# Routed blocks of an expert layer worked in groups of three, and down weights laid over 96 partitions

## The chip, the cores and the metric

The kernel runs on one core of a Trainium2 chip, as one program. Its engines are PE (TensorE: matmuls, with their weight loads shown as PEld), DVE (VectorE), ACT (ScalarE), POOL (GpSimd) and SP (SyncE, which here only issues transfers). The metric is the device time of one execution in microseconds (us). The kernel before took 770.0 us, the median of three runs (769.4 to 772.3).

## The reference, cut to what matters

The program is two transformer layers on x of 4 x 256 tokens of width 256; each layer is a cross-attention and a feed-forward with experts. The change touches only the last part, the experts of the second layer:

```python
# 1024 tokens, H = 256, E = 60 experts, I = 176, TOP_K = 4, all float32
probs = softmax(x @ gate_w.T);  weights, sel = top_k(probs, 4)
cw = zeros((M, E)).at[arange(M)[:, None], sel].add(weights)
def step(acc, ews):                        # scanned over the 60 experts
    w13_e, w2_e, cw_e = ews                # w13: 352 x 256, w2: 256 x 176
    gu_e = x @ w13_e.T
    h = silu(gu_e[:, :I]) * gu_e[:, I:]
    return acc + cw_e[:, None] * (h @ w2_e.T), None
return shared + sparse                     # shared: a dense expert of width 704
```

The kernel does not multiply every token with every expert. It gives each expert slots of token rows, gathers the rows, works them, and scatters the results back.

## The kernel before, in words

The rows sent to the 60 experts are laid out in 53 blocks of 128 rows. Blocks 0 to 44 come in threes for four experts: two blocks with two experts of 64 rows each, then one block with the 32 further rows of all four (`tenants`, line 1697). Blocks 45 to 52 (one round of 8) hold what is over, two units of 64 rows each with an expert known only at run time. Further rounds stand behind a branch at the end and are skipped here.

What one block b goes through in `routed_l1`:

- POOL gathers its 128 rows of 1 KB from `x_rows` into `xg` by an indirect transfer (`fetch_rows`, L1761). There are `XBUF` = 11 such buffers, and fetches run `FETCH` = 8 blocks ahead: POOL's order is fetch(8), send(0), fetch(9), send(1), and so on, so that fetch(b + 8) stands behind send(b - 1) on POOL (L2118 to L2121).
- PE turns the rows (`turn_x`, two transposes, L2138); ACT copies them to SBUF (L2203).
- PE multiplies by the gate and up weights (`gate_up`, L2152). Each expert takes its own columns of the array, 64 or 32 of them, and the products of a block's experts run side by side. ACT applies silu (L2209), and DVE multiplies the halves (L2234).
- PE turns the result in two pieces of 88 columns (`turn_hid`, L2161); ACT copies (L2215).
- PE multiplies by the down weights (`outputs`, L2174), again in column tiles. DVE weights the rows into one of `YBUF` = 4 buffers `yb` (L2245), and POOL scatters them to `y_rows` (L2115).

On PE the blocks are interleaved: step b issues turn_x(b + 3), gate_up(b + 2), turn_hid(b + 1) and outputs(b). So full transposes and column-tiled products alternate, four changes to a block. ACT and DVE follow the same order.

The weights of two experts (a pair) come by two transfers from SP (`load_weights`, L1731): gate and up on 128 partitions, down on 88 partitions (`HC`). A ring holds 12 pairs. Pairs 0 to 11 are loaded before the stage begins; pair q goes out when the last block of pair q - 12 has been multiplied (L2099), two pairs at the end of every three blocks. Pairs 30 to 37, for the last 8 blocks, are loaded expert by expert from a run-time index (`load_further`, L1742).

Behind the last block, POOL waits until all scatters have landed; then the rows of a token are read back, added and stored (`combine_and_store`).

Of the kernel before, what the change touches and what calls it, by code (L numbers as in the profile page):

```python
# [18 lines left out]
P = 128  # L19
D = 256  # L20
# [1638 lines left out]
HC = I1 // 2  # L1659

# [18 lines left out]
XBUF, YBUF, FETCH = 11, 4, 8  # L1679
# [33 lines left out]
def pair_last(q):  # L1713

    return 3 * (q // 2) + 2 if 2 * q < E1 else BASE + q - E1 // 2

# [48 lines left out]
def route_shared_l1(nc, m, io, block, ctx):  # L1765
# [37 lines left out]
    sw13, sw2 = sb("sw13", [KD, 2 * I1S]), sb("sw2", [CH, D])  # L1803
    m.over_ready, m.shared_read, m.y_copied, m.added = sem("over_ready"), silu_done, y_copied, added
# [247 lines left out]
def routed_l1(nc, m, io, block, ctx, out):  # L2052
# [18 lines left out]
    def all_rounds(eng, ahead, step):  # L2071

        for b in range(FIRST - ahead):
            step(b, FIRST)
        eng.wait_ge(m.over_ready, 1)
        units = eng.value_load(m.over[0:1, 0:1], min_val=0, max_val=OVER)

        def further(r):
            end = FIRST + r * ROUND
            if r == FURTHER:  # L2080
                for b in range(end - ahead, end):
                    step(b, end)
                return
            with eng.If(units > 2 * (r + 1) * ROUND):
                for b in range(end - ahead, end + ROUND - ahead):
                    step(b, end + ROUND)
                further(r + 1)
            with eng.Else():
                for b in range(end - ahead, end):
                    step(b, end)  # L2090

        further(0)

    @block.sync
    def _(sp):
# [8 lines left out]
        all_rounds(sp, ROUND, load)  # L2104

    @block.gpsimd
    def _(pool):
# [19 lines left out]
        all_rounds(pool, FETCH, step)  # L2127
# [3 lines left out]
    def _(pe):  # L2131

        def turn_x(b):
            pe.wait_ge(x_loaded[b % XBUF], 16 * (b // XBUF + 1))
            if b >= 2:
                pe.wait_ge(xt_done, b - 1)
            for c in range(KD):
                ins = nc.tensor.transpose(ps[:, 6 + b % 2, c * P:(c + 1) * P], xg[:, b % XBUF, c * P:(c + 1) * P],  # L2138
                                          m.ident[:])
            ins.then_inc(xt_ps, 1)  # L2140

        def gate_up(b):
# [49 lines left out]
        gate_up(0)  # L2192
        gate_up(1)
        turn_hid(0)
        all_rounds(pe, 3, step)

    @block.scalar
    def _(act):
        def copy_x(b):
            act.wait_ge(xt_ps, b + 1)  # L2200
            if b >= 4:
                act.wait_ge(gu_ps, b - 3)
            nc.scalar.copy(xgT[:, b % 4, :], ps[:, 6 + b % 2, 0:D]).then_inc(xt_done, 1)  # L2203

        def silu(b):
            act.wait_ge(gu_ps, b + 1)
            if b >= 2:
                act.wait_ge(hid_done, b - 1)
            nc.scalar.activation(act_g[:, b % 2, :], ps[:, b % 2, 0:I1], ACT.Silu).then_inc(silu_done, 1)  # L2209

        def step(b, end):
            act.wait_ge(ht_ps, b + 1)
            if b >= 2:
                act.wait_ge(y_ps, b - 1)
            nc.scalar.copy(hidT[:, b % 2, :], ps[0:HC, 2 + b % 2, 0:2 * P]).then_inc(ht_done, 1)  # L2215
            if b + 3 < end:
                copy_x(b + 3)
            if b + 2 < end:
                silu(b + 2)

        for b in range(3):
            copy_x(b)
        m.last_copies()
        silu(0)
        silu(1)
        all_rounds(act, 3, step)

    @block.vector
    def _(dve):
        def multiply(b):  # L2230
            dve.wait_ge(silu_done, b + 1)
            if b >= 2:
                dve.wait_ge(ht_ps, b - 1)
# [188 lines left out]
```

## Time and profile before

| | us |
|---|---|
| median of 3 runs (lowest, highest) | 770.0 (769.4, 772.3) |
| the profiled execution, device time | 778.58 |
| span of its trace | 776.8 |
| first product of the routed stage (L2152) | at 584.11 |
| first weight load that waits for the ring | at 596.62 |
| last down product of the stage (L2174) ends | at 751.17 |
| last scatter issued, all landed | at 754.82, 757.31 |

The profiled execution is 8.6 us longer than the median. The trace gives each instruction's start and length on its engine, in microseconds from the start of the span, with its line in the kernel and the tiles it writes and reads. A window row adds up the busy time of each engine in a stretch, with the clock that PE was granted, the mean busy share of the 16 DMA engines and the bytes moved. Idle time is put down to what ended it; "issue" means that the engine waited for nothing that the profile shows.

### The profile page before, as it was taken

Reading aid. Unit: us, or ns where it says so; the run is one execution under the profiler, and the core shown is the slowest. Engines: PE = TensorE matmul, PEld = TensorE weight load, DVE = VectorE, ACT = ScalarE, POOL = GpSimd, SP = SyncE. Lnnn points to the kernel's source line nnn. Section 1 sums busy time; section 2 is a strip of 40 time slices with the busy share of each in tenths; the row PEclk is TensorE's granted clock in tenths of the full one; section 3 lists DMA queues with packets and bytes.
Section 4 is the critical chain, followed back from the end, with each engine's and each line's share of the span. In section 5 each row is a group of like instructions: output and inputs, shape, how many; then the busy total and the mean of one; then the engine's idle time right before and its main releaser. Section 6 shows DMA issues by size and latency. Waiting matters only on the chain. (4 is left out here: it accounts for less than half of the span.)

```text
span 776.8 us, 12603 instructions
## 1 busy us (share of the span) xinstructions
PE 658.9 (85%) x4224; PEld 377.0 (49%) x4224; DVE 427.4 (55%) x1148; ACT 304.9 (39%) x606; POOL 253.7 (33%) x403
## 2 busy tenths in 40 slices
PE   1757888886899999998569999599999999999960
PEld 1543444443676766765335555455664444443430
DVE  4658888863412668868586654469952222222226
ACT  1333778874232223422147676331224332322210
POOL 5350111111144323222102333022365565656530
PEclk9785999998599999999669999689999999999995
DMA  3086211100600556553803310493013999999817
GB/s 114 3 279 187 61 55 57 44 3 1 172 0 14 148 156 183 167 185 108 187 18 109 84 44 1 98 297 126 0 45 103 296 275 280 276 262 292 281 69 270
DMA packets 81807, 103.86 MB, mean 134 GB/s; under 512 B 10093, under 2 KB 56514, under 8 KB 81738
## 3 DMA queue, kind: packets, MB, share of 16 engines
q1 hardware_dynamic: 73930, 85.31, 37.8%
q0 software_dynamic: 5600, 14.02, 6.1%
q10 hardware_dynamic: 2208, 3.67, 1.3%
q8 instruction: 36, 0.59, 0.3%
q14 instruction: 33, 0.27, 0.1%
HBM read 81.17 MB, written 21.65 MB: 132 GB/s over the span
## 5 line engine op out<-in xcount | busy, mean ns | idle before, releaser
L769 DVE TENSOR_REDUCE l_mx<-ps 128x2 f32<-128x512 f32 (+2 forms) x256 | 125.7, 550 | 45.6 <-PE ps L629 45.3
L857 ACT ACTIVATE l_prob<-ps 128x1024 f32<-128x1024 f32 x96 | 98.5, 1027 | 25.8 <-PE ps L659 25.6
L629 PE MATMUL ps<-l_ks,l_qs 48*128 48x256 bf16 (+1 forms) x384 | 71.1, 298 | 28.4 <-DMA l_qs<-l_q_stacks 14.2
L1392 DVE SCALAR_TENSOR_TENSOR xs<-ps,comb,xs 128x256 f32<-128x256 f32 x128 | 55.8, 481 | 59.3 <-PE ps L1052 59.2
L2115 POOL DMA_INDIRECT y_rows<-r_at_blk,row x53 | 52.3, 987 | 59.4 <-DVE r_at_blk L2245 51.9
L674 PE MATMUL ps<-l_prob,v 128*9 128x256 f32 (+1 forms) x768 | 70.3, 389 | 1.1 <-ACT l_prob L857 1.1
L2234 DVE TENSOR_TENSOR r_hot<-r_hot,ps 128x176 f32<-128x176 f32 x53 | 17.9, 338 | 82.5 <-ACT r_hot L2209 43.9
L1141 POOL TENSOR_TENSOR r_ehid<-r_erelu 128x512 f32<-128x512 f32 x32 | 35.5, 1109 | 83.6 <-ACT r_erelu L1245 83.6
L1052 PE MATMUL ps<-f_w,r_ehid 128*128 128x256 f32 x256 | 60.8, 380 | 0.2
L1041 PE MATMUL ps<-xT,f_w 128*128 128x512 f32 x128 | 60.0, 592 | 0.0
L1761 POOL DMA_INDIRECT xg<-x_rows,r_empty x53 | 53.1, 1002 | 18.8 <-issue 14.5
L1052 PEld LDWEIGHTS ps<-f_w,r_ehid 128*128 128x128 f32 x256 | 48.4, 190 | 21.1 <-issue 13.9
L629 PEld LDWEIGHTS ps<-l_ks,l_qs 48*128 48x128 bf16 (+1 forms) x384 | 29.4, 102 | 59.4 <-issue 21.9
L659 PE MATMUL ps<-l_qs,l_ks 50*128 50x256 bf16 (+1 forms) x384 | 56.3, 280 | 0.0
L2245 DVE TENSOR_SCALAR r_at_blk<-ps,row_w 128x256 f32<-128x256 f32 x53 | 25.6, 483 | 51.5 <-remote 24.8
L597 POOL TENSOR_TENSOR attn<-rest,l_rec 128x32 f32<-128x32 f32 x64 | 14.4, 246 | 114.1 <-DVE l_rec L788 114.1
L597 POOL TENSOR_TENSOR l_ctxv<-rest,l_rec 128x64 f32<-128x64 f32 x64 | 17.7, 297 | 85.2 <-DVE l_rec L788 85.2
L2203 ACT COPY r_at_low<-ps 128x256 f32<-128x256 f32 x53 | 19.7, 373 | 59.4 <-PE ps L2138 33.9
L2152 PE MATMUL ps<-ew,r_at_low 128*64 128x352 f32 (+1 forms) x304 | 40.9, 468 | 2.3 <-issue 2.3
L1847 PE MATMUL ps<-xT,r_sw 128*128 128x512 f32 x88 | 41.7, 614 | 0.0
L674 PEld LDWEIGHTS ps<-l_prob,v 128*9 128x9 f32 (+1 forms) x768 | 26.8, 98 | 23.0 <-issue 10.2
L2209 ACT ACTIVATE r_hot<-ps 128x176 f32<-128x176 f32 x53 | 16.9, 320 | 51.9 <-PE ps L2152 25.5
(278 smaller groups left out, 1132.3 us busy)
## 6 DMA issues: line engine op xcount, KB each, us to landing
ew<-in_L_w SPq DMA_DIRECT2D x18, 704.0 KB
ew13b<-in_L_w SPq DMA_DIRECT2D x12, 704.0 KB
f_w<-in_L_w SPq DMA_DIRECT2D x32, 256.0 KB, 2.9
ew<-in_L_w SPq DMA_DIRECT2D x22, 352.0 KB
ew2b<-in_L_w SPq DMA_DIRECT2D x12, 352.0 KB
ew13b<-in_L_w SPq DMA_DIRECT2D x12, 352.0 KB
l_k_stacks<-part SPq DMA_DIRECT2D x8, 384.0 KB, 3.4
l_ks<-l_k_stacks SPq DMA_DIRECT2D x32, 96.0 KB, 2.3
```

The costliest lines, as they stand in the source:

```text
L629: ins = nc.tensor.matmul(ps[:, score_bank(n) + k, qt * S:(qt + 1) * S], qs[row:row + R, u % NBUF, col, qt * P:(qt + 1) * P], ks[row:row + ...
L659: ins = nc.tensor.matmul(ps[:, 2 + 2 * (n % 2) + k, kt * S:(kt + 1) * S], ks[row:row + lay.krows, b, col, kt * P:(kt + 1) * P], qs[row:row ...
L674: ins = nc.tensor.matmul(ps[row:row + W, 6, (c % 2) * S:(c % 2 + 1) * S], v[:, n // UP // GR * QT + kt, head, :], prob[:, n % PROBS, k, kt ...
L769: ins = nc.vector.reduce_max(mx[:, u % 2, :, s, head], one[:, :, lo:hi], AX_X)
L857: nc.scalar.activation(prob[:, n % PROBS, :, :, :].rearrange("p h k q -> p (h k q)"), ps[:, 2 + 2 * (n % 2):4 + 2 * (n % 2), :].rearrange( ...
L1041: ins = nc.tensor.matmul(m.ps[:, n % 2, :], m.f0_up[:, n % WSLOTS, c, :], m.xT[:, c, half * HT:(half + 1) * HT], start=(c == 0), stop=(c = ...
L1052: nc.tensor.matmul(m.ps[:, 2 + t, 0:D], ehid[:, n % 2, t * P:(t + 1) * P], m.f0_down[:, n % WSLOTS, :], start=True, stop=True).then_inc(e_ ...
L1392: v.scalar_tensor_tensor(m.xs[:, i, :], m.ps[:, 2 + t, 0:D], m.comb[:, i, e:e + 1], m.xs[:, i, :], ALU.mult, ALU.add).then_inc(e_added, 1)
L1761: nc.gpsimd.indirect_dma_start(m.xg[:, b % XBUF, :], None, m.x_rows, bass.IndirectOffsetOnAxis(m.token[:, b:b + 1], 0)).then_inc(m.x_loade ...
L1847: ins = nc.tensor.matmul(ps[:, 2 * (q % 2) + a, :], sw13[:, k, own], m.xT[:, k, h * TILES * P:(h + 1) * TILES * P], start=(k == 0), stop=( ...
L2115: nc.gpsimd.indirect_dma_start(m.y_rows, bass.IndirectOffsetOnAxis(m.row[:, b:b + 1], 0), yb[:, b % YBUF, :], None).then_inc(y_sent[b % YB ...
L2152: ins = nc.tensor.matmul(ps[row:row + n, b % 2, 0:2 * I1], xgT[:, b % 4, c * P + row:c * P + row + n], w13[:, s, c, :], start=(c == 0), st ...
```

## The change

Blocks are worked in groups of three (`group_blocks`: 15 groups of three, then 3, 3 and 2 for the round of 8). In step g, PE issues turn_x for the three blocks of group g + 1, turn_hid for the three of group g, then the products that have two experts per block (gate_up of group g + 1, outputs of group g), then those with four experts per block, in the same way. ACT copies and applies silu over two blocks at once and then over the third (`parted`); DVE multiplies likewise, while it weights block by block. PSUM is laid out anew for three blocks at a time: rows turned for a third block share their place with a third block's output, so turn_x of it waits for `y_done` of the group before. `yb` moves to the buffer of the shared expert's weights and has 6 places for 4. Down weights are padded in DRAM and SBUF from 88 to 96 partitions; the products read 88. `FETCH`, `XBUF`, POOL's order and the ring of weights stay.

```diff
 HC = I1 // 2
+HCP = 96
...
-XBUF, YBUF, FETCH = 11, 4, 8
+XBUF, YBUF, FETCH = 11, 6, 8
+GROUPS_ROUND = -(-ROUND // 3)
+FIRST_GROUPS = BASE // 3 + GROUPS_ROUND
...
+def group_blocks(g):
+    if g < BASE // 3:
+        return range(3 * g, 3 * g + 3)
+    r, k = divmod(g - BASE // 3, GROUPS_ROUND)
+    first = BASE + r * ROUND
+    return range(first + 3 * k, min(first + 3 * k + 3, first + ROUND))
+
+
+def spot(b):
+
+    k = b if b < BASE else (b - BASE) % ROUND
+    return k % 3
+
+
+def parted(blocks):
+
+    return [p for p in (blocks[0:2], blocks[2:3]) if len(p)]
+
+
+def halves(b):
+
+    whole, k = (0, b) if b < BASE else divmod(b - BASE, ROUND)
+    done = 2 * (b // 3) if b < BASE else 2 * (BASE // 3) + whole * (2 * (ROUND // 3) + (ROUND % 3 > 0)) + 2 * (k // 3)
+    return done + (1 if spot(b) < 2 else 2)
...
-    xgT = at_low.rearrange("p (j d) -> p j d", j=4)
-    act_g, hid = (hot[:, a * 2 * I1:(a + 1) * 2 * I1].rearrange("p (j n) -> p j n", j=2) for a in range(2))
-    hidT = hot[0:HC, 4 * I1:4 * I1 + 4 * P].rearrange("p (j n) -> p j n", j=2)
-    yb = at_blk[:, 0:YBUF * D].rearrange("p (j d) -> p j d", j=YBUF)
+    xgT = at_low[:, 0:3 * D].rearrange("p (j d) -> p j d", j=3)
+    act_g, hid = (hot[:, a * 3 * I1:(a + 1) * 3 * I1].rearrange("p (j n) -> p j n", j=3) for a in range(2))
+    hidT = hot[0:HC, 6 * I1:6 * I1 + 6 * P].rearrange("p (j n) -> p j n", j=3)
+    yb = m.sw2
...
+    x_ps = (ps[:, 6, 0:D], ps[:, 6, D:2 * D], ps[:, 7, 0:D])
+    hid_ps = (ps[0:HC, 3, 0:D], ps[0:HC, 3, D:2 * D], ps[0:HC, 5, 0:D])
+    out_ps = (ps[:, 4, 0:D], ps[:, 4, D:2 * D], ps[:, 7, 0:D])
...
-        def turn_x(b):
+        def turn_x(b, sent):
             pe.wait_ge(x_loaded[b % XBUF], 16 * (b // XBUF + 1))
-            if b >= 2:
-                pe.wait_ge(xt_done, b - 1)
+            if spot(b) == 2 and sent:
+                pe.wait_ge(y_done, sent)
             for c in range(KD):
-                ins = nc.tensor.transpose(ps[:, 6 + b % 2, c * P:(c + 1) * P], xg[:, b % XBUF, c * P:(c + 1) * P],
+                ins = nc.tensor.transpose(x_ps[spot(b)][:, c * P:(c + 1) * P], xg[:, b % XBUF, c * P:(c + 1) * P],
                                           m.ident[:])
             ins.then_inc(xt_ps, 1)
 
@@ -2143,111 +2178,131 @@
             q = pair_first(b)
             if q is not None:
                 pe.wait_ge(m.ew_loaded[q % (RING // 2)], ring_loads(q))
-            pe.wait_ge(xt_done, b + 1)
-            if b >= 2:
-                pe.wait_ge(hid_done, b - 1)
+            pe.wait_ge(xt_done, halves(b))
             for c in range(KD):
                 for row, n, w in tenants(b):
                     w13, _, s = ring_slot(m, w)
-                    ins = nc.tensor.matmul(ps[row:row + n, b % 2, 0:2 * I1], xgT[:, b % 4, c * P + row:c * P + row + n],
+                    ins = nc.tensor.matmul(ps[row:row + n, spot(b), 0:2 * I1],
+                                           xgT[:, spot(b), c * P + row:c * P + row + n],
                                            w13[:, s, c, :], start=(c == 0), stop=(c == KD - 1))
             ins.then_inc(gu_ps, 1)
 
         def turn_hid(b):
-            pe.wait_ge(hid_done, b + 1)
-            if b >= 2:
-                pe.wait_ge(ht_done, b - 1)
+            pe.wait_ge(hid_done, halves(b))
+            if b == 2:
+                pe.wait_ge(m.y_copied, NT)
             for c in range(2):
-                ins = nc.tensor.transpose(ps[0:HC, 2 + b % 2, c * P:(c + 1) * P],
-                                          hid[:, b % 2, c * HC:(c + 1) * HC], m.ident[:])
+                ins = nc.tensor.transpose(hid_ps[spot(b)][:, c * P:(c + 1) * P],
+                                          hid[:, spot(b), c * HC:(c + 1) * HC], m.ident[:])
             ins.then_inc(ht_ps, 1)
 
         def outputs(b):
-            pe.wait_ge(ht_done, b + 1)
-            if b == 0:
-                pe.wait_ge(m.y_copied, NT)
-            if b >= 2:
-                pe.wait_ge(y_done, b - 1)
+            pe.wait_ge(ht_done, halves(b))
+            if b >= 3:
+                pe.wait_ge(y_done, b - spot(b))
             for c in range(2):
                 for row, n, w in tenants(b):
                     _, w2, s = ring_slot(m, w)
-                    ins = nc.tensor.matmul(ps[row:row + n, 4 + b % 2, 0:D], hidT[:, b % 2, c * P + row:c * P + row + n],
-                                           w2[:, s, c, :], start=(c == 0), stop=(c == 1))
+                    ins = nc.tensor.matmul(out_ps[spot(b)][row:row + n, :], hidT[:, spot(b), c * P + row:c * P + row + n],
+                                           w2[0:HC, s, c, :], start=(c == 0), stop=(c == 1))
             ins.then_inc(y_ps, 1)
 
-        def step(b, end):
-            if b + 3 < end:
-                turn_x(b + 3)
-            if b + 2 < end:
-                gate_up(b + 2)
-            if b + 1 < end:
-                turn_hid(b + 1)
-            outputs(b)
+        def step(g, end):
+            ahead = group_blocks(g + 1) if g + 1 < end else ()
+            for b in ahead:
+                turn_x(b, group_blocks(g)[0])
+            for b in group_blocks(g):
+                turn_hid(b)
+            for many in (2, 4):
+                for b in ahead:
+                    if len(tenants(b)) == many:
+                        gate_up(b)
+                for b in group_blocks(g):
+                    if len(tenants(b)) == many:
+                        outputs(b)
 
         pe.wait_ge(m.table_read, 1)
-        for b in range(3):
-            turn_x(b)
+        for b in group_blocks(0):
+            turn_x(b, 0)
         m.last_outputs()
         pe.wait_ge(m.shared_read, UNITS)
-        gate_up(0)
-        gate_up(1)
-        turn_hid(0)
-        all_rounds(pe, 3, step)
+        for b in group_blocks(0):
+            gate_up(b)
+        all_rounds(pe, FIRST_GROUPS, GROUPS_ROUND, 1, step)
 
...
     @block.scalar
     def _(act):
...
+        def copy_x(bs):
+            p, n = spot(bs[0]), len(bs)
+            act.wait_ge(xt_ps, bs[-1] + 1)
+            if bs[0] >= 3:
+                act.wait_ge(gu_ps, bs[0] - p)
+            nc.scalar.copy(xgT[:, p:p + n, :].rearrange("p j d -> p (j d)"), ps[:, 6 + p // 2, 0:n * D]
+                           ).then_inc(xt_done, 1)
+
...
+        def step(g, end):
+            ahead = group_blocks(g + 1) if g + 1 < end else ()
+            for bs in parted(ahead):
+                copy_x(bs)
+            for bs in parted(group_blocks(g)):
+                copy_hid(bs)
+            for bs in parted(ahead):
+                silu(bs)
+
...
     @block.vector
     def _(dve):
...
+        def weighted(b, last):
+            dve.wait_ge(y_ps, last + 1)
             if b >= YBUF:
                 dve.wait_ge(y_sent[b % YBUF], 16 * (b // YBUF))
+            nc.vector.tensor_scalar(yb[:, b % YBUF, :], out_ps[spot(b)], m.row_w[:, b:b + 1], None,
                                     ALU.mult).then_inc(y_done, 1)
 
-        multiply(0)
-        multiply(1)
-        all_rounds(dve, 2, step)
...
+        def step(g, end):
+            ahead = parted(group_blocks(g + 1) if g + 1 < end else ())
+            for k, bs in enumerate(parted(group_blocks(g))):
+                if k < len(ahead):
+                    multiply(ahead[k])
+                for b in bs:
+                    weighted(b, bs[-1])
+            for bs in ahead[len(parted(group_blocks(g))):]:
+                multiply(bs)
+
...
-        m.ew2 = m.sb("ew2", [HC, EARLY, 2, D])
+        m.ew2 = m.sb("ew2", [HCP, EARLY, 2, D])
...
-            m.ew2b = m.sb("ew2b", [HC, RING - EARLY, 2, D], ctx=scope)
+            m.ew2b = m.sb("ew2b", [HCP, RING - EARLY, 2, D], ctx=scope)
...
-    io["L1_w2"] = rows_together(io.pop("L1_ffn_w2").transpose(0, 2, 1), HC)
+    io["L1_w2"] = np.pad(rows_together(io.pop("L1_ffn_w2").transpose(0, 2, 1), HC), ((0, 0), (0, HCP - HC), (0, 0)))
```

PE in the middle of the stage, before: xg holds gathered rows, r1_hot the silu and its product, r1_at_low the turned rows, ew13 and ew2 the weights; a row's last field is the shape of one matmul.

```order
L2138 MATMUL ps<-ident,xg 128x128 x2
L2152 MATMUL ps<-ew13,r1_at_low 64x352 x4
L2161 MATMUL ps<-ident,r1_hot 88x128 x2
L2174 MATMUL ps<-ew2,r1_hot 32x256 x8
L2138 MATMUL ps<-ident,xg 128x128 x2
L2152 MATMUL ps<-ew13,r1_at_low 32x352 x8
L2161 MATMUL ps<-ident,r1_hot 88x128 x2
L2174 MATMUL ps<-ew2,r1_hot 64x256 x4
```

The same place after, one whole step:

```order
L2173 MATMUL ps<-ident,xg 128x128 x6
L2195 MATMUL ps<-ident,r1_hot 88x128 x6
L2185 MATMUL ps<-ew13,r1_at_low 64x352 x8
L2206 MATMUL ps<-ew2,r1_hot 64x256 x8
L2185 MATMUL ps<-ew13,r1_at_low 32x352 x8
L2206 MATMUL ps<-ew2,r1_hot 32x256 x8
```

Two blocks before had eight stretches of four kinds; three blocks after have six stretches, and all turns of rows stand at the head of the step.

PE at the end of the stage, before:

```order
L2138 MATMUL ps<-ident,xg 128x128 x2
L2152 MATMUL ps<-ew13,r1_at_low 64x352 x4
L2161 MATMUL ps<-ident,r1_hot 88x128 x2
L2174 MATMUL ps<-ew2b,r1_hot 64x256 x4
L2152 MATMUL ps<-ew13,r1_at_low 64x352 x4
L2161 MATMUL ps<-ident,r1_hot 88x128 x2
L2174 MATMUL ps<-ew2b,r1_hot 64x256 x4
L2161 MATMUL ps<-ident,r1_hot 88x128 x2
L2174 MATMUL ps<-ew2,r1_hot 64x256 x8
```

The same place after:

```order
L2173 MATMUL ps<-ident,xg 128x128 x4
L2195 MATMUL ps<-ident,r1_hot 88x128 x6
L2185 MATMUL ps<-ew13,r1_at_low 64x352 x8
L2206 MATMUL ps<-ew2b,r1_hot 64x256 x12
L2195 MATMUL ps<-ident,r1_hot 88x128 x4
L2206 MATMUL ps<-ew2,r1_hot 64x256 x8
```

The gate and up products of the last two blocks now stand ahead of the outputs of the three blocks before them.

## Rows read from the trace of the kernel before

**Rows 1.** Windows of core 0: window, length, busy (x count) per engine, clock, DMA share, GB/s
```profile
512.00:524.00 12.00, 12.00 (x45) 5.63 (x44) 9.69 (x35) 4.42 (x7) 3.94 (x3) 0.99 1.05 263
527.00:533.00 6.00, 6.00 (x19) 3.42 (x18) 5.72 (x10) 1.07 (x2) 1.78 (x1) 1.00 0.72 240
600.00:735.00 135.00, 131.32 (x1062) 55.03 (x1058) 33.15 (x82) 39.72 (x124) 81.31 (x83) 1.00 0.97 282
```

**Rows 2.** Waits from 590 to 762 us: engine line waited for, us, times, longest
```profile
PEld ps L2138 <- issue: 19.3, 49, 0.4
...
PE ps L2152 <- issue: 2.7, 4, 2.0
```

**Rows 3.** Timeline, 655 to 675 us, one block on PE: start, us, engine, instruction
```profile
656.57 0.44 PE L2138 MATMUL ps<-ident,xg 128*128 128x128 f32 x2
...
656.94 1.41 PE L2152 MATMUL ps<-ew,r_at_low 128*64 128x352 f32 x8
...
658.27 0.42 PE L2161 MATMUL ps<-ident,r_hot 128*88 128x128 f32 x2
...
658.62 1.08 PE L2174 MATMUL ps<-ew,r_hot 88*64 88x256 f32 x8
...
659.64 0.44 PE L2138 MATMUL ps<-ident,xg 128*128 128x128 f32 x2
659.75 0.48 DVE L2245 TENSOR_SCALAR r_at_blk<-ps,row_w 128x256 f32<-128x256 f32 x1 [0.68 <-PE ps L2174]
```

**Rows 4.** Timeline, 655 to 675 us, from a weighted block to POOL's transfers
```profile
655.41 0.48 DVE L2245 TENSOR_SCALAR r_at_blk<-ps,row_w 128x256 f32<-128x256 f32 x1 [2.45 <-remote]
...
656.18 0.99 POOL L2115 DMA_INDIRECT y_rows<-r_at_blk,row  x1 [1.63 <-DVE r_at_blk L2245]
...
657.47 0.97 POOL L1761 DMA_INDIRECT xg<-x_rows,r_empty  x1 [0.30 <-issue]
...
658.74 0.99 POOL L2115 DMA_INDIRECT y_rows<-r_at_blk,row  x1 [0.30 <-issue]
```

**Rows 5.** Timeline, 572 to 612 us, the first blocks on PE
```profile
580.92 0.60 PE L2138 MATMUL ps<-ident,xg 128*128 128x128 f32 x4
...
584.11 2.59 PE L2152 MATMUL ps<-ew,r_at_low 128*64 128x352 f32 x16
...
586.63 0.42 PE L2161 MATMUL ps<-ident,r_hot 128*88 128x128 f32 x2
```

**Rows 6.** DMA issues from 500 to 536 us: KB each, median us to landing
```profile
ew13b<-in_L_w SPq DMA_DIRECT2D x6, 704.0 KB
ew2b<-in_L_w SPq DMA_DIRECT2D x6, 352.0 KB
...
r_sw<-in_L_shared_w SPq DMA_DIRECT2D x3, 256.0 KB, 7.2
r_sw<-in_L_shared_w SPq DMA_DIRECT2D x1, 128.0 KB, 6.5
```

**Rows 7.** Line 1761, the row fetches: ns min/median/max, first and last start
```profile
L1761 POOL DMA_INDIRECT xg<-x_rows,r_empty x53: 952/970/1873, 566.6 to 731.7; - x53
```

**Rows 8.** Timeline of the sync engine: its weight loads
```profile
596.62 21.65 SPq L1731 DMA_DIRECT2D ew<-in_L_w  x12
...
719.18 10.27 SPq L1742 DMA_DIRECT2D ew<-in_L_w  x8
```

**Rows 9.** Chain of waits at the stage's end: start, us, what
```profile
743.28 0.37 PE ps L2138 x2
...
746.35 2.02 issue
...
750.13 1.04 PE ps L2174 x8
...
754.82 2.49 DMA y_rows<-r_at_blk,row
```

More of the change, by code:

```diff
@@ L1803, in route_shared_l1 @@
     sw13, sw2 = sb("sw13", [KD, 2 * I1S]), sb("sw2", [CH, D])
+    m.sw2 = sw2
     m.over_ready, m.shared_read, m.y_copied, m.added = sem("over_ready"), silu_done, y_copied, added
@@ L2069, in routed_l1, with all_rounds @@
     ps = m.ps
-    def all_rounds(eng, ahead, step):
-        for b in range(FIRST - ahead):
-            step(b, FIRST)
+    x_ps = (ps[:, 6, 0:D], ps[:, 6, D:2 * D], ps[:, 7, 0:D])
+    hid_ps = (ps[0:HC, 3, 0:D], ps[0:HC, 3, D:2 * D], ps[0:HC, 5, 0:D])
+    out_ps = (ps[:, 4, 0:D], ps[:, 4, D:2 * D], ps[:, 7, 0:D])
+    def all_rounds(eng, first, size, ahead, step):
+        for n in range(first - ahead):
+            step(n, first)
         eng.wait_ge(m.over_ready, 1)
@@ L2078, in further @@
         def further(r):
-            end = FIRST + r * ROUND
+            end = first + r * size
             if r == FURTHER:
-                for b in range(end - ahead, end):
-                    step(b, end)
+                for n in range(end - ahead, end):
+                    step(n, end)
                 return
             with eng.If(units > 2 * (r + 1) * ROUND):
-                for b in range(end - ahead, end + ROUND - ahead):
-                    step(b, end + ROUND)
+                for n in range(end - ahead, end + size - ahead):
+                    step(n, end + size)
                 further(r + 1)
             with eng.Else():
-                for b in range(end - ahead, end):
-                    step(b, end)
+                for n in range(end - ahead, end):
+                    step(n, end)
         further(0)
@@ L2103, in load @@
                     load_further(sp, m, io, 2 * q)
-        all_rounds(sp, ROUND, load)
+        all_rounds(sp, FIRST, ROUND, ROUND, load)
     @block.gpsimd
@@ L2126, in _ @@
         pool.wait_ge(m.added, NT)
-        all_rounds(pool, FETCH, step)
+        all_rounds(pool, FIRST, ROUND, FETCH, step)
         nc.gpsimd.memset(settled_mark, 0.0).then_inc(y_settled, 1)
@@ L2205, in silu @@
[L2205 to L2219, printed above, removed]
@@ L2221, in _, with copy_hid @@
-        for b in range(3):
-            copy_x(b)
+        def copy_x(bs):
[5 more added lines that the diff above has]
+                           ).then_inc(xt_done, 1)
+        def copy_hid(bs):
+            p, n = spot(bs[0]), len(bs)
+            act.wait_ge(ht_ps, bs[-1] + 1)
+            if bs[0] >= 3:
+                act.wait_ge(y_ps, bs[0] - p)
+            src = ps[0:HC, 3, 0:2 * D] if p == 0 else hid_ps[p]
+            nc.scalar.copy(hidT[:, p:p + n, :].rearrange("p j d -> p (j d)"), src).then_inc(ht_done, 1)
@@ new lines, in silu @@
+        def silu(bs):
+            p, n = spot(bs[0]), len(bs)
+            act.wait_ge(gu_ps, bs[-1] + 1)
+            if bs[0] >= 3:
+                act.wait_ge(hid_done, halves(bs[0] - p - 1))
+            nc.scalar.activation(act_g[:, p:p + n, :], ps[:, p:p + n, 0:I1], ACT.Silu).then_inc(silu_done, 1)
+        def step(g, end):
[6 more added lines that the diff above has]
+                silu(bs)
@@ L2223, in _ @@
+        for bs in parted(group_blocks(0)):
+            copy_x(bs)
         m.last_copies()
-        silu(0)
-        silu(1)
-        all_rounds(act, 3, step)
+        for bs in parted(group_blocks(0)):
+            silu(bs)
+        all_rounds(act, FIRST_GROUPS, GROUPS_ROUND, 1, step)
     @block.vector
     def _(dve):
[L2230 to L2233, printed above, removed]
-            nc.vector.tensor_tensor(hid[:, b % 2, :], act_g[:, b % 2, :], ps[:, b % 2, I1:2 * I1], ALU.mult
-                                    ).then_inc(hid_done, 1)
@@ L2237, in _, with multiply @@
-        m.clear_sems(dve)
-        def step(b, end):
-            if b + 2 < end:
-                multiply(b + 2)
-            dve.wait_ge(y_ps, b + 1)
+        def multiply(bs):
+            p, n = spot(bs[0]), len(bs)
+            dve.wait_ge(silu_done, halves(bs[0]))
+            if bs[0] >= 3:
+                dve.wait_ge(ht_ps, bs[0] - p)
+            nc.vector.tensor_tensor(hid[:, p:p + n, :], act_g[:, p:p + n, :], ps[:, p:p + n, I1:2 * I1], ALU.mult
+                                    ).then_inc(hid_done, 1)
@@ new lines, in step @@
+        def step(g, end):
[7 more added lines that the diff above has]
+                multiply(bs)
+        for bs in parted(group_blocks(0)):
+            multiply(bs)
+        all_rounds(dve, FIRST_GROUPS, GROUPS_ROUND, 1, step)
```

7 lines of the change are left out of this document (1 added, 6 removed).

## The prediction

> **What bounds the kernel now.** The change touches only the stretch from the first routed product at 584.11 us [rows 5] to the last scatter [rows 9], so I read that alone. First the windows, for who is busy: from 600 to 735 us PE works 131.3 of 135 us at full clock, and the 16 DMA engines are busy 0.97 of the time at 282 GB/s, while DVE, ACT and POOL have room [rows 1]. Two things are close to full at once. Then the waits, for which of the two ends last: the row turns never stood over 0.4 us, the products waited 2.7 us in all, and neither waited for a DMA [rows 2]. So PE sets the pace, and the weights come in time. Then the timeline, for what PE spends on a block: from one row turn to the next 3.06 us, made of 0.37 (turn of the rows), 1.33 (gate and up), 0.35 (turn of the hidden) and 1.01 (down) [rows 3]. Three blocks cost 9.19.
>
> The stage runs from 584.11 to 751.17 [rows 5, 9]. Its pieces are 2.52 for the first two gate-up products, 0.35, fifty blocks with all four parts (153.0), and 2.69 + 1.36 + 1.01 for the last blocks without turns: 160.9. With the stand of 2.0 us at the branch [rows 9] that is 162.9; the other 4.2 us are scattered stalls.
>
> **The change, part by part.** *Trains on PE.* Four row turns in a train took 0.60 [rows 5], 0.15 each, where a pair alone takes 0.37, so a change of kind costs 0.07 there. Six of them: 0.97. Six hidden turns at the same pace: 0.90. Two gate-up products in a train took 2.52 (584.11 to 586.63, rows 5) for 2 x 1.33, so the change into products costs about 0.15. I take it once for each train and let the down products follow without it, at 1.01 - 0.15 = 0.86. A step of three blocks is then 0.97 + 0.90 + 2.52 + 1.72 + 1.33 + 0.86 = 8.30 instead of 9.19. The bounds are 9.19, if every change still costs, and 7.9, if none does. Were PE still the bound, 17 steps would save 15 us.
>
> *What is late next: the gathered rows.* FETCH stays 8 while the rows are turned earlier, all at the head of a step. The last block turned in step g is 3g + 5; its fetch stands on POOL behind the send of block 3g - 4, the last of group g - 2. Counted from the start of step g - 2: the two-expert outputs end at 0.97 + 0.90 + 2.52 + 1.72 = 6.11; DVE starts 0.12 later (a product from 658.62 that takes 1.01, DVE at 659.75, rows 3); POOL's send follows 0.77 after DVE's start, and each POOL transfer is 1.28 behind the last [rows 4]. Send, fetch, send, fetch, send, fetch: the third fetch goes out at 7.00 + 5 x 1.28 = 13.4. It must have landed when step g has turned two blocks, at two steps plus 0.67. So two steps are 12.7 plus the landing time, and a step is 6.37 plus half of it.
>
> The trace does not show that landing time. From below it is 2.5, what the last scatter, also 128 KB, took with nothing else moving [rows 9]. From above it is 11.6: the last fetch went out at 731.7 and its rows were turned at 743.28 without a wait [rows 7, 9]. Nearest are loads of 128 and 256 KB while DMA was full, 6.5 and 7.2 [rows 6]. I take 7.0, since DMA is full here too, with both kinds of queue. A step is then 9.87, longer than the 9.19 of today; the two are equal at 5.6 us. PE waits 1.57 in each step, with the hidden turns and all the products queued behind the row turn, and with them ACT, DVE and the next sends.
>
> *Weights.* A pair is 704 + 352 KB [rows 6] and becomes 704 + 384. The loads that wait for the ring begin at 596.62 [rows 8], 26 pairs, after the third block as now. They are 26 x 1.114 = 29.0 MB, and about 90 row transfers of 128 KB add 11.8: 40.8 MB, at 282 GB/s 145 us, to 741. With the steps below, the last pairs are wanted from 743 on, so they are just covered. If the cover goes, the outputs of three blocks stand behind the wait, which they did not before.
>
> When 88-partition loads drain alone, the mean share is 0.72, which is 11.5 of 16 engines, at 240 GB/s; with all at work it was 263 [rows 1]. The spread over 96 may thus be worth up to a tenth of the rate; in the stage the share is already 0.97, so I count nothing, and the bounds on the end of the loads are 730 and 752 (at 305, which is 282 x 1.05 / 0.97, and at 263 GB/s).
>
> The Trainium skill (DMA: Bandwidth & Descriptors, section "Why a DMA increments its semaphore by 16 and not by 1") says that a load is split over the largest number up to 16 that divides its outer dimension: 11 for 88 partitions and 16 for 96. The 0.72 agrees. By that rule alone the fullest engine carries 44 + 24 KB a pair for 44 + 32 before, an estimate of a tenth less, and the loads would end near 732.
>
> *Six send buffers for four.* DVE's wait for a scatter two groups back has over 10 us to spare; nothing. Wider ACT and DVE instructions replace narrow ones on engines with room; nothing, as long as PE waits for rows.
>
> *The sum, in the profiled execution.* From 584.11: three gate-up products 3.85. Steps 0 to 2, whose rows are fetched before the loads fill DMA, 3 x 8.30 = 24.9. Steps 3 to 15, 13 x 9.87 = 128.3. Step 16, which turns two blocks only, 0.67 + 0.90 + 2.52 + 2.58 = 6.7. The branch 2.0. The last two blocks 2.9 with the copy. That is 168.7, against 162.9 now. Of the stalls of 4.2 I let 3.0 stay, as those ahead of the sends are not hidden by the row wait: 171.7 against 167.1, 4.6 more. Behind the last product the scatter goes out 0.12 + 0.77 + 1.28 = 2.2 later instead of 3.65 (751.17 to 754.82, rows 9): 1.4 less. The change costs 3.2 us. The profiled execution, 778.6 with a span of 776.8, would take 781.8; it stands 8.6 above the median of 770.0, and I carry the difference over as it is: 773.
>
> **Rivals.** *The rows land quickly.* If all 16 engines share the weights evenly and a fetch lands within 4 us, a step is PE's 8.30. Then the weights are the bound, since PE would want the last pairs at 722. With their end at 735 the tail is 735 + 1.3 (gate-up of the last block) + 2.6 (three outputs) + 2.0 + 2.9 + 2.2 = 746 for the last scatter, against 754.8: 9 us less, or 6 with loads that end at 738; 761 to 767, about 764. For it: 0.72 above. Against it: 0.97, and six POOL transfers in a row.
>
> *Bursts land later.* Sends and fetches now come six in a row, beside loads that run on all 16 engines instead of 11. At 9 us for a landing a step is 10.87, thirteen of them add 13, and the time is 786; at 8 it is 780. It is the forecast's loop with a larger price, and it decides from about 7.5 on. For it: DMA is full either way. Against it: 6.5 and 7.2 were measured on a full queue.
>
> The Trainium skill (same page, "Queues, rings and completion order") says that a DMA engine takes a whole packet of several descriptors from one ring before it turns to the next, so that a gather waits behind the weights' packets. By it more engines with packets mean more late parts of a gather; no run here shows it.
>
> *The trains save nothing.* If each product still pays its change, POOL's first send comes about 0.7 later, a step is 6.7 plus half the landing, 10.2, and the time is 777. For it: no row shows a down product behind a gate-up one. Against it: the pair of gate-up products.
>
> *It cancels.* At a landing of 6.5 a step is 9.62, thirteen steps give back 3.3, and the time is 770. That is the lower part of the forecast's own range.
>
> **How the numbers follow.** About 0.5% (3.85 us) is what a measurement of this kernel can tell from no change. The forecast's loop, with landings from 6.3 to 7.4 us, gives 769 to 776 and has 0.48: 0.31 of it under 773.9, 0.17 over. Quick rows have 0.24, of which 0.22 is faster by more than 0.5% and 0.02 is not. Bursts have 0.18, all slower. Trains that save nothing have 0.10, of which 0.05 is slower. That makes 0.22 faster, 0.38 within, 0.40 slower. The range reaches from the middle of the quick-rows case, 764, to the lower part of the bursts, 781.
>
> **What would show it.** In the profile after: row turns that stand about 1.5 us in each step from the fourth on, at the third block; steps of 9.6 to 10 us; POOL's transfers in runs of six; no wait for weights before the last two groups. PE's step without waits should be 8.3, with the down products of two blocks at 1.7 behind their gate-up products. In a window where only down weights drain, DMA's share should no longer stop at 0.72. The prediction is wrong if the row turns do not wait, or if the products wait for weights in many steps; then the landing time or the rate was the wrong term.

## The result, and the profile after

The change makes the kernel slower: 791.4 us in the median (788.4 to 797.1, 4 runs) beside 771.2 us of the kernel before (769.4 to 772.6, 4 runs), a ratio of 1.0249 with a 95% interval of 1.0204 to 1.0293. The forecast was 773 with a range of 764 to 781. The profiled execution after took 788.4 us with a span of 786.5.

Windows of the kernel after, first the stretch of [rows 1], then four pieces of two neighbouring steps. Columns as in [rows 1]:

```profile
600.00:735.00 135.00, 114.03 (x930) 59.82 (x932) 26.62 (x60) 32.55 (x76) 74.67 (x76) 0.89 0.92 279
...
656.44:664.63 8.19, 8.08 (x80) 4.39 (x76) 2.22 (x5) 2.53 (x6) 5.89 (x7) 1.00 0.90 268
664.63:668.73 4.10, 0.88 (x8) 0.40 (x5) 0.48 (x1) 0.59 (x1) 3.19 (x4) 0.91 1.05 320
668.73:675.10 6.37, 6.37 (x24) 3.31 (x26) 0.00 (x0) 1.23 (x3) 1.71 (x2) 0.52 1.03 303
675.10:679.11 4.01, 4.01 (x50) 1.91 (x46) 1.74 (x4) 0.78 (x2) 0.99 (x2) 1.00 0.60 158
```

PE, which worked 131.3 of 135 us before, works 114.0, and its granted clock, 1.00 throughout before, is 0.89 in the mean. The four pieces show where: a step without a wait takes 8.19 us at the full clock; in the next one PE works 0.88 of 4.10 us, then runs 6.4 us at 0.52, close to the lower of its two levels (1.2 of 2.4 GHz), and only then at 1.00 again. DMA is no longer full, 0.92.

The waits of the kernel after, 590 to 762 us, that answer to [rows 2] (line 2173 is the row turn):

```profile
PEld ps L2173 <- DMA xg<-x_rows,r_empty: 24.0, 13, 3.0
PE ps L2173 <- DMA xg<-x_rows,r_empty: 20.9, 13, 2.7
```

Before, no wait of PE in the stage was for a DMA. Now 13 row turns wait for gathered rows, 20.9 us in all, and no product waits for a weight.

PE's timeline of the same two steps, the answer to [rows 3] (2173 row turns, 2195 hidden turns, 2185 gate and up, 2206 down; in brackets the idle time before and what ended it):

```profile
656.44 1.18 PE L2173 MATMUL ps<-ident,xg 128*128 128x128 f32 x6
657.45 0.82 PE L2195 MATMUL ps<-ident,r_hot 128*88 128x128 f32 x6
658.20 2.59 PE L2185 MATMUL ps<-ew,r_at_low 128*64 128x352 f32 x16
660.62 1.90 PE L2206 MATMUL ps<-ew,r_hot 88*64 88x256 f32 x16
662.45 1.39 PE L2185 MATMUL ps<-ew,r_at_low 128*32 128x352 f32 x16
663.65 1.05 PE L2206 MATMUL ps<-ew,r_hot 88*32 88x256 f32 x16
664.63 0.44 PE L2173 MATMUL ps<-ident,xg 128*128 128x128 f32 x2
667.23 0.44 PE L2173 MATMUL ps<-ident,xg 128*128 128x128 f32 x2 [2.16 <-DMA xg<-x_rows,r_empty]
668.73 0.69 PE L2173 MATMUL ps<-ident,xg 128*128 128x128 f32 x2 [1.06 <-DMA xg<-x_rows,r_empty]
669.21 1.49 PE L2195 MATMUL ps<-ident,r_hot 128*88 128x128 f32 x6
670.63 4.63 PE L2185 MATMUL ps<-ew13b,r_at_low 128*64 128x352 f32 x16
675.10 1.90 PE L2206 MATMUL ps<-ew,r_hot 88*64 88x256 f32 x16
```

The first step is the trains alone, 656.44 to 664.63. In the second, the second and third block's rows are late (2.16 and 1.06 us of standing), the hidden turns take 1.49 instead of 0.82, and the same gate-up train 4.63 instead of 2.59, with nothing in front of it. Such steps alternate over the loaded stretch: from the step that starts at 598.97 to the one at 728.71 there are six pairs of steps, 21.6 us each, 10.8 a step. The step at 598.97 is the third of the stage.

The chain of waits through one turn of the loop, the answer to [rows 4] (start, duration, what):

```profile
647.35 0.59 PE ps L2173 x2
647.94 1.28 PE ps L2195 x6
649.22 3.37 PE ps L2185 x16
652.59 1.76 PE ps L2206 x16
654.37 0.50 DVE r_sw L2288
655.13 0.99 POOL y_rows L2150
...
661.58 7.11 DMA xg<-x_rows,r_empty
668.73 0.69 PE ps L2173 x2
...
764.42 2.51 DMA y_rows<-r_sw,row
```

Between 655.13 and 661.58 stand the six POOL transfers, 1.29 us apart. The loop is the one of the prediction: turn, products, send, fetch, landing, turn. The last scatter goes out at 764.42, where [rows 9] has 754.82.

### The profile page after: what moved, and what is told of

Same layout as the page of the kernel before. It is cut to its first block and busy times, and to the rows that moved or that the text cites. A ratio compares the mean times of both kernels' runs of the same rounds, so it can differ in the third digit from the quotient of the medians.

```text
span 786.5 us, 12357 instructions
## 1 busy us (share of the span) xinstructions
PE 651.7 (83%) x4224; PEld 389.8 (50%) x4224; DVE 423.0 (54%) x1130; ACT 297.8 (38%) x552; POOL 254.3 (32%) x403
## 5 line engine op out<-in xcount | busy, mean ns | idle before, releaser
L2281 DVE TENSOR_TENSOR r_hot<-r_hot,ps 128x352 f32<-128x352 f32 (+1 forms) x35 | 15.1, 432 | 128.8 <-ACT r_hot L2256 128.8
L2150 POOL DMA_INDIRECT y_rows<-r_sw,row x53 | 52.5, 990 | 73.8 <-DVE r_sw L2288 63.2
L2256 ACT ACTIVATE r_hot<-ps 128x352 f32<-128x352 f32 (+1 forms) x35 | 13.8, 393 | 84.0 <-PE ps L2185 84.0
L2185 PE MATMUL ps<-ew13b,r_at_low 128*64 128x352 f32 (+1 forms) x240 | 39.5, 542 | 0.0
L2173 PE MATMUL ps<-ident,xg 128*128 128x128 f32 x106 | 20.5, 298 | 21.8 <-DMA xg<-x_rows,r_empty 20.9
```

What stands on the lines that cost most here:

```text
L2150: nc.gpsimd.indirect_dma_start(m.y_rows, bass.IndirectOffsetOnAxis(m.row[:, b:b + 1], 0), yb[:, b % YBUF, :], None).then_inc(y_sent[b % YB ...
L2185: ins = nc.tensor.matmul(ps[row:row + n, spot(b), 0:2 * I1], xgT[:, spot(b), c * P + row:c * P + row + n], w13[:, s, c, :], start=(c == 0) ...
```

## The experiments

All ratios are to the kernel before, run on the same chip in the same session. Its median was 771.2 to 775.3 us in the different sessions, so kernels of this table are best compared by their ratios. "11 ahead" means that POOL fetches the rows of block b + 11 in front of the send of block b, where the changed kernel fetches b + 8.

| kernel | us, median | ratio, 95% interval |
|---|---|---|
| after | 791.4 | 1.0249 (1.0204 to 1.0293) |
| e1: after, 11 ahead | 772.6 | 1.0012 (0.9978 to 1.0046) |
| e6: after, 9 ahead | 773.8 | 1.0011 (0.9976 to 1.0047) |
| e7: after, useless work added | 783.8 | 1.0127 (1.0067 to 1.0186) |
| e2: after, 88 partitions | 795.5 | 1.0318 (1.0235 to 1.0400) |
| e3: before, 96 partitions | 769.9 | 0.9992 (0.9965 to 1.0019) |
| e4: before, 11 ahead | 771.6 | 1.0015 (0.9979 to 1.0051) |
| e5: e1, 88 partitions | 775.7 | 1.0029 (0.9994 to 1.0064) |
| e8: e1, early gate-up weights | 769.5 | 0.9946 (0.9913 to 0.9980) |
| e9: e8, two kinds of semaphores | 763.3 | 0.9878 (0.9837 to 0.9918) |
| e10: e9, useless work added | 763.9 | 0.9888 (0.9844 to 0.9931) |
| e11: before, early gate-up weights | 775.1 | 1.0012 (0.9973 to 1.0052) |
| e12: e9, 88 partitions | 763.5 | 0.9852 (0.9825 to 0.9879) |

**e1, the loop taken away.** The ring of row buffers has 11 places, of which the changed kernel uses 8:

```
+LEAD = 11
...
-            if b + FETCH < end:
-                fetch(b + FETCH)
+            if b + LEAD < end:
+                fetch(b + LEAD)
...
-        all_rounds(pool, FIRST, ROUND, FETCH, step)
+        for b in range(FETCH, LEAD):
+            fetch(b)
+        all_rounds(pool, FIRST, ROUND, LEAD, step)
```

> The grouped kernel with row fetches issued 11 blocks ahead instead of 8 (three more fetches before the first send; the ring has 11 buffers). Theory (a loop of fetch behind send bounds the step, and each wait also costs clock): each fetch starts about one step, some 8 us, earlier, the row turns find their rows, steps fall from a mean of 10.7 us to the 8.2 us that a step without a wait takes, and the kernel takes 752 to 766 us; the granted clock of the stage is 1.00. Rival W (the 96-partition weight loads crowd the queues): steps stay over 9.5 us with waits on weights, 780 to 791 us. Rival P (the grouped order is itself longer on TensorE): 785 to 791 us.

Windows of e1, then what PE's gate-up products (here line 2188) waited for from 590 to 735 us:

```profile
600.00:680.00 80.00, 78.88 (x736) 43.00 (x737) 21.22 (x49) 24.98 (x59) 57.63 (x59) 1.00 1.05 297
680.00:735.00 55.00, 48.09 (x358) 25.04 (x350) 10.91 (x27) 12.20 (x29) 22.57 (x23) 0.84 0.95 270
```

```profile
PE ps L2188 <- DMA ew2b<-in_L_w: 3.4, 1, 3.4
PE ps L2188 <- DMA ew<-in_L_w: 3.1, 2, 2.9
```

No row turn waits for rows any more, and up to 690 us the steps start 8.19 to 8.20 us apart at a clock of 1.00. That gives back the whole loss, 18.9 us: the lead of the fetches was its cause. Both rivals, with 780 us or more, are out. It gives no gain over the kernel before, and the expected 752 to 766 was missed: now that PE is quicker, DMA is full from 620 us on, the products wait for weights from 693 us on, and the clock falls there (0.84 from 680 to 735 us). The last weight lands at 731.3 us and the last scatter goes out at 743.97.

**e6, a smaller dose.** The same edit with `LEAD = 9`.

> The grouped kernel with row fetches 9 blocks ahead, a dose between 8 and 11. Theory: the third fetch of a step comes one send earlier, 2.6 us, so two steps take 10.7 (from the start of step g-2 to the fetch) + 7.0 landing - 0.7 = 17.0 us and the mean step 8.5 us, against 8.2 and 10.7; total waits for rows in the row turns fall from 45 us to under 8 us, granted clock of 600 to 690 us at least 0.97, time 768 to 777 us. Rival (a threshold elsewhere, only the full depth helps): over 782 us.

Waits of e6 for rows, 590 to 735 us, and its window:

```profile
PEld ps L2176 <- DMA xg<-x_rows,r_empty: 11.7, 12, 1.6
PE ps L2176 <- DMA xg<-x_rows,r_empty: 8.8, 11, 1.4
```

```profile
600.00:680.00 80.00, 73.78 (x692) 39.73 (x688) 20.00 (x46) 23.21 (x54) 53.66 (x55) 1.00 1.05 300
```

One more block of lead makes the fetch one POOL pair earlier. From the step at 594.62 to the one at 708.04, thirteen steps take 8.72 us each; 8.5 was expected from a landing of 7.0, and the chain shows landings of 6.8 to 8.3. The loop's arithmetic holds, and the rival, over 782 us, is out. The waits are longer than expected: the 45 us in the expectation add the row of PE (20.9) and that of its weight loads (24.0), which overlap. By the same sum e6 has 20.5, where under 8 was expected; PE alone fell from 20.9 to 8.8. Row waits of up to 1.4 us leave the clock at 1.00. The longer steps hardly show in the time, 773.8 beside 772.6 of e1: here too, products wait for weights at the end of the stage, 5.6 us in two waits.

**e7, work added to separate the wait from the clock.**

```
+FILL = 10
...
         def step(g, end):
             ahead = group_blocks(g + 1) if g + 1 < end else ()
+            for _ in range(FILL if ahead else 0):
+                nc.tensor.transpose(x_ps[0][:, 0:P], m.ident[:], m.ident[:])
```

> The grouped kernel (8 ahead) with ten more transposes of the unit matrix on TensorE at the head of each step, work of no use, 1.7 us at the full clock. Theory (a wait also costs the clock behind it): the work falls into the wait; two steps take 13.3 + 1.7 + 7.0 - 0.7 - 1.7 = 19.6 us, a step 9.8 to 9.9 us with a granted clock near 1.00, so in spite of the added work the kernel is faster than without it, 775 to 785 us. Rival (the clock costs nothing that the loop of fetch and send does not hide): 790 us or more, up to 820 us if the work simply adds.

Windows of e7, four steps (the second and fourth have a wait):

```profile
655.92:664.91 8.99, 8.99 (x89) 5.51 (x87) 2.22 (x5) 2.39 (x6) 5.88 (x6) 1.00 1.02 309
664.91:675.48 10.57, 9.42 (x89) 5.46 (x88) 2.22 (x5) 2.59 (x6) 5.88 (x6) 1.00 0.99 314
675.48:684.46 8.98, 8.98 (x88) 5.51 (x87) 2.22 (x5) 2.39 (x6) 5.88 (x6) 1.00 1.00 301
684.46:695.08 10.62, 9.43 (x89) 5.48 (x88) 2.22 (x5) 2.59 (x6) 5.87 (x6) 1.00 0.98 287
```

The chain of e7 through the same part of the loop as the chain of the kernel after (2174 row turns, 2196 hidden turns, 2186 gate and up):

```profile
647.32 0.44 PE ps L2174 x2
647.76 0.66 PE ps L2196 x6
648.41 2.52 PE ps L2186 x16
650.93 1.75 PE ps L2207 x16
...
659.91 6.92 DMA xg<-x_rows,r_empty
666.88 0.44 PE ps L2174 x2
```

With useless work the kernel is 7.6 us faster, and the intervals of the two ratios do not overlap. The rival, 790 us or more, is out. Ten transposes lengthen a step without a wait by 0.8 us (8.98 for 8.20), less than the 1.7 expected: the row turns start 1.15 us behind them, and the six turns then take 0.82 us instead of 1.18. The clock stays at 1.00, and one turn of the loop takes 19.56 us (647.32 to 666.88) where the kernel after needs 21.38 (647.35 to 668.73): hidden turns 0.66 for 1.28, gate-up 2.52 for 3.37, turn 0.44 for 0.59, while the landing is 6.92 for 7.11. So a wait can cost more than its length: in the kernel after, the work behind it runs at the lower clock, and that work is on the loop that produces the next wait.

The Trainium skill (TensorE: Matmul & The Clock Gate, section "HAM oscillation — how this bites in real kernels") describes a loop of this kind: where products wait for a DMA between short stretches of work, each stretch starts at the lower clock, and the loss is paid at every turn. The trace agrees in kind, with 0.52 over the 6.4 us behind the wait, but not at every wait: those of e6, up to 1.4 us, left the clock at 1.00.

**e2 to e4, the parts of the change alone.** e2 undoes the spread (`HCP = HC`, so 88 partitions); e3 makes it alone, in the kernel before; e4 is the control for e1, the lead of 11 in the kernel before.

> The grouped kernel with the down weights on 88 partitions as before. Theory: the loop stays; if a landing is 1 us shorter a pair of steps is 1 us shorter, so 781 to 792 us. Rival W: the whole loss is gone, 765 to 772 us. Rival P: 785 to 792 us.

> The kernel before with only the down weights laid over 96 partitions. Theory: rows are fetched early enough there, so 768 to 774 us. Rival W: 780 to 792 us. Rival P: no change, 768 to 774 us.

> The kernel before with row fetches 11 blocks ahead. Theory: the loop does not bound the ungrouped step, whose first row turn is three blocks ahead of its products, so 766 to 772 us. A rival, that rows are late in both kernels: 755 to 764 us.

Waits of e2 for rows (590 to 762 us), then the windows of e3 and of e4, each in a fence of its own:

```profile
PE ps L2173 <- DMA xg<-x_rows,r_empty: 22.7, 14, 2.6
```

```profile
600.00:735.00 135.00, 135.00 (x1100) 56.88 (x1096) 36.14 (x88) 46.50 (x132) 82.68 (x85) 1.00 0.98 288
```

```profile
600.00:735.00 135.00, 135.00 (x1102) 57.16 (x1102) 36.46 (x89) 46.88 (x133) 80.46 (x82) 1.00 0.95 285
```

The grouping alone has the whole loss: with 88 partitions rows wait as long, 22.7 us. The kernel's 795.5 is over the 792 at which the theory's range ended, so shorter landings from the narrow layout, which it had allowed for, aren't there. Rival W is out, and rival P with it, since e1 gives the loss back in the grouped order. The spread alone changes nothing, and neither does the lead where blocks go one by one: PE works all of 135 us.

**e5 and e8 to e12, what bounds the grouped kernel once its rows are in time.**

> The grouped kernel with row fetches 11 blocks ahead and the down weights on 88 partitions. With 11 ahead and 96 partitions the steps take 8.19 us until TensorE overtakes the weights at 690 us and waits for them. Theory (the stage then ends with the weight transfers; 88 partitions carry 3% fewer bytes at a rate about 3 to 5% lower, as 276 to 288 GB/s beside 284 to 307 in the runs of the kernel before): within 5 us of 96 partitions, 768 to 778 us, first wait for weights before 700 us. Rival (the wider spread is what lets the weights keep up): 778 to 788 us.

The narrow layout lets the last weight land at 736.7 us beside 731.3 in e1, but the times (775.7 and 772.6, overlapping intervals) don't tell the two apart. The first wait is in the step that starts at 682 us, and the time is in the theory's range.

e8 lets the sync engine replace gate and up weights when their last reader is done, a step ahead of the down products (both loaders take the kind of weights as an argument). Its core:

```
-        def load(b, end):
+        def load(b, used, dram):
...
-                sp.wait_ge(y_ps, pair_last(q - RING // 2) + 1)
+                sp.wait_ge(used, pair_last(q - RING // 2) + 1)
...
+        def step(b, end):
+            load(b, gu_ps, ("L1_w13",))
+            if b >= BEHIND:
+                load(b - BEHIND, y_ps, ("L1_w2",))
...
```

with `BEHIND = 3`. e9 gives each kind a semaphore of its own, so that `gate_up` waits for the first kind, and `outputs` has a wait for the second:

```
-                pe.wait_ge(m.ew_loaded[q % (RING // 2)], ring_loads(q))
+                pe.wait_ge(m.ew_loaded["L1_w13"][q % (RING // 2)], ring_loads(q))
...
         def outputs(b):
+            q = pair_first(b)
+            if q is not None:
+                pe.wait_ge(m.ew_loaded["L1_w2"][q % (RING // 2)], ring_loads(q))
```

> The grouped kernel, 11 ahead, and each pair's gate and up weights are replaced as soon as its gate-up products are done, instead of waiting for its down products, which come a step later; the down weights follow three blocks behind. Theory (with rows in time the stage ends with the weight transfers, and those start late: 66 GB/s from 575 to 590 us): the transfers start about one step, 8 us, earlier, the last weights land 4 to 8 us earlier, 762 to 769 us, faster than both kernels. Rival (bandwidth is full and the order is worth nothing, or the down weights now come last): 769 to 776 us.

> As the grouped kernel with 11 ahead and the gate and up weights replaced early, and now with semaphores of their own for the two kinds of weights, so that gate-up products wait for the gate and up weights alone and the down products for the down weights. In the run with one semaphore the last weight landed at 728 us (731 without the early replacement), but gate-up products waited for down weights from 682 us on and TensorE ran the rest at 0.55 to 0.79 of its clock. Theory (those waits and the clock behind them took the gain): first wait later than 690 us, last row sent by 745 us, 762 to 768 us. Rival (bandwidth alone sets it, the waits only move): 768 to 773 us.

Of e8, the waits in PE's timeline and the last window (2200 is gate and up):

```profile
710.85 2.61 PE L2200 MATMUL ps<-ew13b,r_at_low 128*64 128x352 f32 x8 [4.82 <-DMA ew2b<-in_L_w]
715.91 2.61 PE L2200 MATMUL ps<-ew13b,r_at_low 128*64 128x352 f32 x8 [2.45 <-DMA ew2b<-in_L_w]
```

```profile
700.00:740.00 40.00, 32.51 (x218) 17.28 (x214) 6.92 (x18) 7.14 (x17) 11.52 (x12) 0.74 0.67 190
```

Of e9, the same:

```profile
716.91 1.76 PE L2200 MATMUL ps<-ew13b,r_at_low 128*64 128x352 f32 x8 [2.12 <-DMA ew13b<-in_L_w]
...
726.40 1.40 PE L2200 MATMUL ps<-ew,r_at_low 128*64 128x352 f32 x8 [1.05 <-DMA ew<-in_L_w]
```

```profile
700.00:740.00 40.00, 30.86 (x232) 16.86 (x230) 8.52 (x20) 7.77 (x18) 14.85 (x17) 0.89 0.66 197
```

In e8 the transfers start earlier (from 590 to 620 us 319 GB/s, 279 in e1), and the last weight lands at 728 us, 3 us earlier, where 4 to 8 were expected. But gate-up products wait for down weights that they don't read, 7.3 us in two waits, and the clock from 700 to 740 us is 0.74. The time, 769.5, falls just outside the theory's range and into the rival's. With a semaphore for each kind, e9, 3.1 us of waits remain, the first at 715 us, the clock there is 0.89, the last row is sent at 739.9 us, and the kernel takes 763.3 us, as its theory had it: 1.2% faster than the kernel before, with 1 outside the interval. The first such wait of e8 stands at 706 us; the 682 in the expectation of e9 is e5's and was put to the wrong run.

> The same with three useless transposes of the unit matrix, 0.5 us, at the head of each step. Theory (TensorE runs ahead of the weights, waits and loses its clock; paced, it waits less and keeps it): steps of 8.7 us, granted clock of 700 to 740 us over 0.85, 762 to 768 us, no slower than without the added work although that is 9 us over the stage. Rival (the added work simply adds where weights are in time): 3 to 9 us slower than without it.

Inconclusive. Three transposes lengthen a step by 0.02 us only (8.22 for 8.20), as the gap within the row turns takes them up, so the pace was not changed, and nothing follows on pacing.

> The kernel before (blocks one by one, 88 partitions, 8 ahead) with the gate and up weights replaced early. Theory (TensorE's 9.19 us for three blocks bounds it and no product waits for a weight): no change, 768 to 775 us, so that early replacement pays only where the blocks are grouped. Rival (weights bound it too): 762 to 768 us.

No gain without the grouping, as expected: 775.1 us, at the very end of the theory's range. But the reason given does not hold in the profiled execution (778.1 us). A gate-up product (line 2164) waits there for a down weight, behind 729.67 us, and the clock from 728 to 752 us is 0.79:

```profile
PE ps L2164 <- DMA ew2b<-in_L_w: 2.1, 1, 2.1
```

This kernel keeps one semaphore for both kinds, so it is the control of e8, not of all of e9; the order block by block with two kinds of semaphores was not run.

> The fastest version so far (grouped, 11 ahead, gate and up weights replaced early, two kinds of semaphores; 763.3 us) with the down weights back on 88 partitions. Theory (the spread is worth nothing while rows bound the step, but once the weights end the stage it is worth the difference seen in the last landing, 731 against 737 us with 11 ahead): the last weight lands 4 to 7 us later and the kernel is 3 to 7 us slower than on 96 partitions, 766 to 770 us. Rival (the 3% fewer bytes make up for it): 761 to 765 us.

The theory fell and its rival held: 763.5 beside 763.3, with overlapping intervals of the ratios. The last weight lands 2 us later (733.4, 731.3), and the time doesn't show it. The wide layout is worth nothing measurable in any of the three pairs (after and e2, e1 and e5, e9 and e12).

## Why the prediction was wrong

**Trains on PE: right.** A step without a wait takes 8.19 us where 8.30 was forecast and 9.19 spent before. The rival that the trains save nothing is out.

**What is late next: right in mechanism, wrong in size, and this is the step that failed.** Rows are late at the third block of a step, through the send two groups back, with landings of 6.2 to 7.7 us in the chain of waits where 7.0 was taken; the median of all fetches from 600 to 720 us is 7.0. They are late at the second block too (2.16 of the 3.22 us in the step shown), and from the third step on, not the fourth. But the step was priced at 9.87 us with PE at its full clock all along, so that a wait cost its length alone, and it takes 10.8. Of what stands between a row's turn and the next fetch, the hidden turns were put at 0.90 and the first gate-up train at 2.52; in the chain they take 0.66 to 1.28 and 3.4 to 4.6. e7 shows the price to be right for the clock that it assumed: a turn of its loop measures 19.56 us, two steps were to take 12.7 + 7.0 = 19.7. The rest is the clock behind the waits. From the first hidden turn to the first down product, the seven steps with a long wait take 13.3 us more, added up, than the same work takes in steps without one; thirteen steps at 10.8 instead of 9.87 are 12.

The forecast also spread the wait evenly, 1.57 in each step. The loop reaches over two steps, so one group's wait need not be its neighbour's: the waits gathered in every second step, and were long there.

**Weights and the spread: right on the outcome.** The loads ended at 734.5, forecast 741, and nobody waited for them; e1 shows that this cover goes once a step takes 8.2 us. The spread over 96 partitions shows at the end of the burst of loads ahead of the stage, in two windows of the kernel after:

```profile
526.00:530.00 4.00, 4.00 (x13) 2.22 (x12) 3.90 (x4) 0.80 (x2) 0.97 (x1) 1.00 0.92 252
530.00:536.00 6.00, 6.00 (x21) 3.47 (x19) 5.83 (x14) 1.44 (x3) 2.53 (x2) 1.00 0.05 15
```

DMA's share is 0.92 and then next to nothing, where [rows 1] had a drain at 0.72. That agrees with the rule of the Trainium skill that the prediction cites (DMA: Bandwidth & Descriptors, section "Why a DMA increments its semaphore by 16 and not by 1"). The spread decides no time here (e3, e12).

**Six send buffers, wider copies: right**, nothing waits there.

**The sum.** Two terms make up the miss of 18 us. First gate-up to last scatter was to take 171.7 + 2.2 = 173.9 us and took 185.4 (579.0 to 764.4): 11.5, about what the clock took. The other is the base. The profiled execution of before has 170.7 us for this stretch [rows 5, 9], while e3 and e4, which change no time, both have 164.2. From one row turn to the next a block takes 3.06 us in e3 and e4; in the profiled execution of before, eight blocks take 3.3 to 4.2, together 5.8 more, and what held them is not settled. (e11 has 171.0, but keeps 3.06 up to 729.67 and loses its time behind that, at its wait for a weight.) The change was summed against a long execution and carried to the median "as it is". Against 164.2 the same 173.9 would have been 9.7 us slower, not 3.2: about 780.

**The rivals.** Quick rows did not happen; its next bound did, once e1 put the rows in time. Weights then end the stage, from 731.3 us to a scatter at 743.97, where that case had 735 and 746. It is no gain, since e3 and e4, in the order of before, send theirs at 744.9 and 747.0. Bursts that land later came nearest in time, 786 us at a landing of 9, for the wrong reason: the median fetch takes 7.0 us, as it does in e3, where fetches go out one by one, and it was the work behind the wait that slowed. That it cancels, at 770, did not happen.

## What to carry to other kernels

When work is regrouped, count every prefetch lead again from the new place of its issue to the new place of its use: eight blocks were plenty one by one and too few by threes, and one more gave the loss back (e6). A wait on TensorE can cost its length and the clock of what follows; if that work feeds the next wait, price the loop at the lower clock as well. A faster engine then meets the next bound (here the weights): release each buffer at its own last reader, with its own semaphore, so that nobody waits for what it doesn't read (772.6 us in e1, 769.5 and 763.3 in e8 and e9).

## What the hardware showed that was not expected

- Standing of 2.16 and 1.06 us, with two row turns between, cost a stretch of 6.4 us at a clock of 0.52. In e7 the longest wait for rows was 2.0 us and in e6 1.4, and the clock of both stayed at 1.00 from 600 to 680 us.
- Useless products ahead of a wait made a kernel faster: 783.8 us for 791.4.
- Between its last load ahead of a branch and its first behind it, the sync engine issues nothing for 8 us. Its loads in e1 (line 1762 ahead, 1773 behind):

```profile
654.42 21.75 SPq L1762 DMA_DIRECT2D ew<-in_L_w  x7
684.46 0.38 SPq L1773 DMA_DIRECT2D ew13b<-in_L_w  x1
```

  The first group ends at 676.17, and the products that the next load waits for ended at 665.2. In e3 the gap is 669.68 to 677.94, in the kernel after 681.61 to 689.57. DMA's backlog covered it in e1, where 311 GB/s were moved from 676.17 to 684.46; what the engine waits for was not tried.
